# Layer-2 features from projected keys and queries in row blocks, one table of steps per batch, and earlier weight loads

## What is computed

```python
q = (x @ Wq + bq).reshape(B, S, H, hd).transpose(0, 2, 1, 3)
...
x_proj = jnp.einsum('bhsd,dm->bhsm', x, random_matrix)   # hd = 8, m = 32, H = 16
return (jax.nn.elu(x_proj) + 1.0) * INV_SQRT_M
...
kv = jnp.einsum('bhsm,bhsd->bhmd', k_prime, v)
k_sum = k_prime.sum(axis=2)
out = jnp.einsum('bhsm,bhmd->bhsd', q_prime, kv)
...   # divided by q_prime . k_sum, then @ Wo + bo
```

## Time and profile before

| | us |
|---|---|
| median of 3 runs | 527.77 |
| lowest, highest | 526.52, 531.72 |
| the profiled execution | 527.63 |
| its span, first to last instruction | 525.8 |
| TensorE busy | 481.0 |
| VectorE busy | 386.0 |
| ScalarE busy | 224.6 |
| POOL busy | 106.5 |

### The profile page before, as it was taken

How to read it: one execution, slowest core, us unless ns; L and a number is a source line. 1 busy time by engine, 2 the same in 40 slices (tenths; PEclk the granted TensorE clock), 3 DMA queues, 4 the chain that set the end, 5 groups by cost and what they waited for, 6 DMA issues and landing times. The chain is left out here.

```text
span 525.8 us, 7943 instructions
## 1 busy us (share of the span) xinstructions
PE 481.0 (91%) x2903; PEld 232.8 (44%) x2903; DVE 386.0 (73%) x994; ACT 224.6 (43%) x302; POOL 106.5 (20%) x101
## 2 busy tenths in 40 slices
PE   8889899999999999989979979999999999988772
PEld 3333233334333343333335545556557456545471
DVE  6398888887898888798629796974678466655553
ACT  2306657667766656656841222231332232233110
POOL 9880427006440010000100002000011001212020
PEclk9999999999999999999999999998999799879756
DMA  4854342224322333200132113112111000000000
GB/s 155 259 142 156 90 123 92 91 70 112 115 91 70 93 86 113 66 1 22 23 80 82 60 42 100 42 60 60 41 42 51 30 20 1 21 1 0 22 20 20
DMA packets 24878, 36.31 MB, mean 69 GB/s; under 512 B 2684, under 2 KB 16258, under 8 KB 24834
## 3 DMA queue, kind: packets, MB, share of 16 engines
q1 hardware_dynamic: 24840, 35.81, 23.3%
HBM read 24.07 MB, written 11.53 MB: 68 GB/s over the span
## 5 line engine op out<-in xcount | busy, mean ns | idle before, releaser
L1092 DVE TENSOR_REDUCE negmax<-psum 128x1 f32<-128x512 f32 x256 | 169.6, 687 | 34.0 <-PE psum L521 33.8
L805 ACT ACTIVATE probs<-psum 128x1024 f32<-128x1024 f32 x128 | 127.7, 1022 | 60.1 <-PE psum L537 57.7
L521 PE MATMUL psum<-KS,QS 125*128 125x512 bf16 x256 | 98.5, 385 | 7.4 <-DVE negmax L1092 4.1
L556 PE MATMUL psum<-probs,VA 128*32 128x256 f32 x1024 | 80.5, 390 | 0.4 <-ACT probs L805 0.4
L537 PE MATMUL psum<-QS,KS 128*128 128x512 bf16 x256 | 76.0, 380 | 0.1
L784 PE MATMUL psum<-xT,late 128*128 128x512 f32 x144 | 73.3, 634 | 0.0
L521 PEld LDWEIGHTS psum<-KS,QS 125*128 125x128 bf16 x256 | 24.5, 96 | 82.0 <-DVE negmax L1092 39.9
L448 POOL TENSOR_SCALAR var<-mv 128x4 f32<-128x4 f32 x16 | 4.3, 270 | 262.6 <-DVE mv L992 262.5
L915 ACT ACTIVATE QS<-psum 128x512 f32<-128x512 f32 x36 | 21.5, 597 | 65.2 <-PE psum L784 65.2
L771 PE MATMUL psum<-late,QS 128*128 128x128 f32 x288 | 40.6, 285 | 5.7 <-DVE QS L956 3.0
L1254 DVE SCALAR_TENSOR_TENSOR QS<-QS,psum 128x512 f32<-128x512 f32 x36 | 24.5, 680 | 26.1 <-ACT QS L915 26.1
(11 more groups left out here) (148 smaller groups left out, 590.0 us busy)
## 6 DMA issues: line engine op xcount, KB each, us to landing
stack_dram<-parts SPq DMA_DIRECT2D x24, 384.0 KB, 3.3
cw<-w_dram SPq DMA_DIRECT2D x32, 256.0 KB, 3.3
KS<-stack_dram SPq DMA_DIRECT2D x16, 288.0 KB
QS<-stack_dram SPq DMA_DIRECT2D x16, 288.0 KB
late<-in_late SPq DMA_DIRECT2D x8, 346.5 KB, 4.4
res<-in_x SPq DMA_DIRECT2D x4, 256.0 KB, 3.3
w_dram<-wT SPq DMA_DIRECT2D x4, 256.0 KB, 4.4
out_y<-KS SPq DMA_DIRECT2D x4, 256.0 KB, 2.2
```

Source lines behind the costliest of these rows:

```text
L521: mm(sm_bank(u)[:, :], QS[b % 2][0:KROW, h, qt * P:(qt + 1) * P], KS[b % 2][0:KROW, h, :], start=True, stop=True).then_inc(sm_full, 1)
L556: last_ = mm(ps[6][32 * j:32 * j + 32, q], VA[b % 2][:, kt, h, :], probs[:, n % 2, j, q], start=(kt == 0 and half == 0), stop=(kt == NT - ...
L805: fn(probs[:, n % 2, 2 * hf:2 * hf + 2, :], psum[:, 2 * hf:2 * hf + 2, :], ACT.Exp, scale=float(DH) ** -0.5).then_inc(exp_done, 1)
L1092: V.tensor_reduce(out=negmax[:, G % 4, i:i + 1], in_=sm_bank(u)[:, :], axis=X, op=ALU.max, negate=True).then_inc(sm_free, 1)
```

## The change

It does five things.

1. `wR`, `kb`, the split and the three bias DMAs go. Each batch gets `kp` and `qp`: keys and queries, projected (128x512 matmuls with `wk1`, `wq1`), evacuated by ScalarE with the bias into `kT`, `qT`.
2. K and Q tiles are made in pairs. K m and m+1: four matmuls, of 64 rows of `kT` with 256 columns of `rbd`, row block 0 into the first bank and 1 into the second, for two token tiles. Q m and m+1: two matmuls, each of the 32 rows of a head group, 128 features by 512 tokens.
3. ScalarE takes exp without bias and, as a second pass, identity with bias 1 into `kone` or `qone`; VectorE reads both from SBUF. A bank is free after ScalarE's second pass.
4. The rounds become one table `steps` for a batch, laid at 9 (n+1); where batches share a step, the later batch stands first. `x2T` is at 4, `kp` and `qp` at 5, K at 6 and 7, Q at 8 and 9, `KV` 9, `O` 10, `OT` 11, `AT` 12, `Y1` 14, `norm2` 15, `x3T` 17, `lg` 18, `ghT` 21, `Y2` 22, `norm3` 23. What is beyond step 35 is the tail, in this order, and crowded banks end with step 35.
5. The first three weight tiles are loaded right after `combine` of batch 0 (window 112).

```diff
-            wqT=D, wkT=D, wv1=D, wo1=D, rbd=H * M1, bq_rep=P, bk_rep=P, bv1_row=D, bo1_row=D, mask=HW,
+            wq1=D, wk1=D, wv1=D, wo1=D, rbd=H * M1, bq_col=1, bk_col=1, bv1_row=D, bo1_row=D, mask=HW,
...
-        wqR, wkR, bias_row = (probs[:, 0, i, :] for i in range(3))
...
+        qT, kT = probs[:, 0, 0, :], probs[:, 0, 1, :]
+        qone, kone = probs[:, 0, 2:4, :], probs[:, 1, 0:2, :]
...
-        a_round = (("K", 0, 0), ("AT", 1, 0), ("K", 0, 1), ("Y1", 1, 0), ("K", 0, 2), ("ghT", 2, 0), ("K", 0, 3),
-                   ("V", 0, 0), ("norm2", 1, 0), ("Y2", 2, 0), ("Q", 0, 0), ("Q", 0, 1), ("x3T", 1, 0), ("Q", 0, 2),
-                   ("norm3", 2, 0), ("lg", 1, 0), ("Q", 0, 3), ("KV", 0, 0), ("O", 0, 1), ("O", 0, 0), ("OT", 0, 1),
-                   ("OT", 0, 0))
-        round_at = (4, 4, 5, 5, 5, 6, 6, 7, 7, 7, 8, 8, 9, 9, 9, 10, 10, 11, 12, 12, 12, 12)
...
+        steps = ((0, "chunk", 0), (1, "norm1", 0), (4, "x2T", 0), (5, "kp", 0), (5, "qp", 0), (6, "K", 0), (6, "K", 1),
+                 (7, "K", 2), (7, "K", 3), (7, "V", 0), (8, "Q", 0), (8, "Q", 1), (9, "Q", 2), (9, "Q", 3), (9, "KV", 0),
+                 (10, "O", 1), (10, "O", 0), (11, "OT", 1), (11, "OT", 0), (12, "AT", 0), (14, "Y1", 0), (15, "norm2", 0),
+                 (17, "x3T", 0), (18, "lg", 0), (21, "ghT", 0), (22, "Y2", 0), (23, "norm3", 0))
+        for n in reversed(range(NB)):
+            for at, kind, c in steps:
+                beside[PAIRS * (n + 1) + at].append((kind, n, c))
...
-            for j in range(NB * EP):
-                if j == 12:
-                    sp.wait_ge(kb_done, 2)
-                    for i in range(3):
-                        sp.dma_start(bias_stack[i:i + 1, :, :], bias_parts[0:1, :, i, :]).then_inc(ks_ld, 16)
+                        if a == 0:
+                            for j in range(CW):
+                                load_weights(j)
+            for j in range(CW, NB * EP):
...
                 if kind == "K":
-                    mm(o[:, :], tile_of(m), wkR[:, :], start=True, stop=False)
-                    last_ = mm(o[:, :], onesb[:, 0:P], bias_stack[:, 0, :], start=False, stop=True)
+                    other = ("K", b, m + 1)
+                    wait_free(pe, other)
+                    for t in range(2):
+                        for r, out_ in enumerate((o, bank_of(other))):
+                            half = slice(64 * r, 64 * (r + 1))
+                            last_ = mm(out_[:, 256 * t:256 * (t + 1)], kT[half, (m + t) * P:(m + t + 1) * P],
+                                       c_["rbd"][half, 256 * r:256 * (r + 1)], start=True, stop=True,
+                                       tile_position=(64 * r, 0))
...
                 if kind == "Q":
-                    mm(o[:, :], wqR[:, m * P:(m + 1) * P], xT[:, b * T:(b + 1) * T], start=True, stop=False)
-                    last_ = mm(o[:, :], bias_stack[:, 1, m * P:(m + 1) * P], onesb[:, :], start=False, stop=True)
+                    other = ("Q", b, m + 1)
+                    wait_free(pe, other)
+                    for c, out_ in ((m, o), (m + 1, bank_of(other))):
+                        rows_ = slice(HW * c, HW * (c + 1))
+                        last_ = mm(out_[:, :], c_["rbd"][rows_, c * P:(c + 1) * P], qT[rows_, :], start=True, stop=True,
+                                   tile_position=(HW * c, 0))
...
-                    fn(ek_[:, i % 2, :], bank_of(u)[:, :], ACT.Exp, bias=minus1[:, 0:1]).then_inc(expk_done, 1)
+                    fn(ek_[:, i % 2, :], bank_of(u)[:, :], ACT.Exp)
+                    fn(kone[:, i % 2, :], bank_of(u)[:, :], ACT.Identity, bias=plus1[:, 0:1]).then_inc(expk_done, 1)
...
-                    V.scalar_tensor_tensor(out=KF[:, m, :], in0=ek_[:, i % 2, :], scalar=1.0, in1=bank_of(u)[:, :],
+                    V.scalar_tensor_tensor(out=KF[:, m // 2 * 2:m // 2 * 2 + 2, 256 * (m % 2):256 * (m % 2 + 1)], in0=ek_[:, i % 2, :], scalar=1.0, in1=kone[:, i % 2, :],
```

More of the change, by code:

```diff
@@ L96, in program @@
         cw = sb("cw", [P, CW, T])
-        onesb = sb("onesb", [3, T], BF16)
         warm_in = sb("warm_in", [P, T], BF16)
@@ L221, in program @@
-        round_at = (4, 4, 5, 5, 5, 6, 6, 7, 7, 7, 8, 8, 9, 9, 9, 10, 10, 11, 12, 12, 12, 12)
-        for n in range(NB):
-            w = PAIRS * (n + 1)
-            for at, kind in ((0, "chunk"), (1, "norm1"), (3, "x2T")):
-                beside[w + at].append((kind, n, 0))
-            if n + 1 < NB:
-                for (kind, back, c), at in zip(a_round, round_at):
-                    if n >= back:
-                        beside[w + at].append((kind, n - back, c))
+        steps = ((0, "chunk", 0), (1, "norm1", 0), (4, "x2T", 0), (5, "kp", 0), (5, "qp", 0), (6, "K", 0), (6, "K", 1),
[3 rows of a table added]
@@ L230, in program @@
+        for n in reversed(range(NB)):
+            for at, kind, c in steps:
+                beside[PAIRS * (n + 1) + at].append((kind, n, c))
         layer2 = [s for one in beside[NB * PAIRS:] for s in one]
         del beside[NB * PAIRS:]
-        crowded = {s for one in beside for s in one} | set(layer2)
-        for n in range(last, NB + 2):
-            layer2 += [(kind, n - back, c) for kind, back, c in a_round if 0 <= n - back < NB]
+        crowded = {s for one in beside for s in one}
@@ L237, in program @@
         uses = [[] for _ in range(8)]
-        in_misc = ("rope", "val", "max", "heads", "attnT", "proj", "resT", "gate", "combine", "wR", "kb", "x2T")
+        in_misc = ("rope", "val", "max", "heads", "attnT", "proj", "resT", "gate", "combine", "x2T")
         uses[MISC] = [s for one in [[("val", 0, 0), ("max", 0, 0)]] + slots for s in one if s[0] in in_misc]
@@ L246, in program @@
             uses[5].append(("y_e", b, 0))
-        bank_for = {"K": 2, "Q": 0, "V": 4, "KV": 5, "O": 5, "OT": 5, "AT": 7, "Y1": 4, "x3T": 7, "lg": 5, "ghT": 7, "Y2": 6, "x2T": 7}
+        bank_for = {"kp": 3, "qp": 1, "K": 2, "Q": 0, "V": 4, "KV": 5, "O": 5, "OT": 5, "AT": 7, "Y1": 4, "x3T": 7, "lg": 5, "ghT": 7, "Y2": 6, "x2T": 7}
         swap = 0
@@ L486, in _ @@
                 pool.wait_ge(init_pool, i + 1)
-            link(nc.gpsimd.memset(onesb[:, :], 1.0))
             nc.gpsimd.memset(VK[:, :, :, :], 1.0).then_inc(init_pool, 1)
```

77 lines of the change are left out of this document (39 added, 38 removed).

## The result

| | time, median | profiled execution | span | mean granted clock |
|---|---|---|---|---|
| before | 527.14 us (4 runs, 524.46 to 531.72) | 527.63 us | 525.8 us | 0.952 |
| changed | 521.47 us (4 runs, 519.22 to 523.43) | 519.63 us | 517.8 us | 0.926 |

The ratio is 0.9896, with a 95% interval of 0.9848 to 0.9944: 5.7 us are gained, where 14 were forecast. The number lies in the range of 505 to 527, but the forecast saw over twice the gain. Ratios are taken to runs of the kernel before on the same chip, and leave out runs over 1.5% above the fastest of their kernel.

The account below looks back on a forecast made before the run. It took TensorE matmul time to bound the expert stage and latency, one batch's chain of small steps, the tail; 19.0 us saved less 4.9 lost gives 14.1 less, 513.5, said as 514 us, range 505 to 527.

Parts of the forecast that it names:

- Row blocks overlap: K and Q pairs: row blocks run side by side like O's column blocks, 1.00 us a pair, gaining 9.8 us.
- row blocks don't overlap: Rival for K and Q pairs: 1.86 us a pair, time 525 us; chance 0.15.
- The expert stage: From the first gate_e to the last up_e: features, folded weights, sooner loads and table together save 19.0 us.
- Features and folded weights: Expert stage: pairs with projections save 9.8 us, dropping wR and kb saves 3.4 + 2.6 us.
- table and loads: Expert stage: sooner weights save 2.7 us; the new step table saves 2.4 and costs 0.4 and 1.5.
- the clock falls more often: Rival: each expert-stage pair brings a place at 1.2 GHz behind it, 19.8 us, time 533.3 us; chance 0.10.
- The tail is no worse: Rival: full clock in lg, Y2 and Y1 and room for gates in the tail, time 507 us; chance 0.18.
- The tail: After the last up_e, one batch's chain of small steps: five pieces together 4.9 us worse.
- third piece: Tail, KV 3 to attn: lg 2 now in between, 3.7 + 0.9 + 3.5 + 4.0 = 12.1 us, 2.3 worse.
- second piece: Tail, x2T 3 to KV 3: pairs at ScalarE's pace, 18.2 us instead of 23.5, 5.3 better.
- `KV` itself at 1.2 GHz in the tail: Rival: gaps from ScalarE's pace make KV 7.3 instead of 3.7 us, twice, time 521 us; chance 0.12.
- ScalarE's second pass: Extra identity per tile: covered in the expert stage; in the tail pairs follow at 2 x 1.2 us of ScalarE.

Follow-up runs that it names:

- e3: The kernel before with only the first three weight tiles loaded sooner; 523.32 us, ratio 0.9893.
- e4: The changed kernel's features (projections, pairs, two ScalarE passes, no folded weights) in the rounds and with the weight loads of the kernel before; 526.25 us, ratio 0.9863.
- a0: The changed kernel run once more, unaltered, which gives its second profile; 523.63 us, ratio 0.9928.
- e1: The changed kernel with only the tail's list put back in the order of the kernel before; 517.42 us, ratio 0.9774.
- e6: The changed kernel with full matmuls for the tail's pairs and the tail in the order of the kernel before; 509.97 us, ratio 0.9664.
- e5: The changed kernel with full 128-row matmuls for the tail's pairs, row blocks kept in the expert stage; 515.04 us, ratio 0.9748.
- e13: The changed kernel with only the tail's Q pairs as full 128-row matmuls, its K pairs still in row blocks; 513.61 us, ratio 0.9787.
- e9: The changed kernel with one full matmul, whose result is overwritten, ahead of each row-block pair of the tail; 522.26 us, ratio 0.9915.
- e7: The changed kernel without ScalarE's second pass; VectorE reads the tile from PSUM and the added 1 is left out; 528.66 us, ratio 0.999.
- e11: e6 with lg moved to PSUM bank 3 and short bf16 filler matmuls in TensorE's remaining tail gaps; 496.77 us, ratio 0.942.
- e14: The kernel before with only lg moved from bank 5 to PSUM bank 3; 527.66 us, ratio 1.0026.

## Why the prediction was right or wrong

**Row blocks overlap: right.** A pair is 1.05 to 1.06 us, forecast 1.00 from the column blocks of `O`. (By the 3.07 times of the Trainium skill, TensorE: Matmul & The Clock Gate, Part 3: Packing small matmuls, the estimate was 1.12: this trace lies between the two.) The rival "row blocks don't overlap" fell.

**The expert stage: right, and a little small.** Forecast -19.0; measured -24.3, and -21.1 in the second profile, which has 10.2 us at 1.2 GHz like before's. Step 11's `gate_e` starts 35.8 us after the stage's start instead of 46.0, so 10.2 sooner where some 9 were forecast; the weights alone are 2.7 of them in `e3`, as forecast. The last `up_e` ends at 419, forecast 422, although the stage began 2.5 us late. Single terms within the other 7.5 us were not measured one by one, but three profiles with the same 10.2 us at 1.2 GHz split the stage: 172.9 before, 159.1 in `e4`, 151.8 in `a0`. Features and folded weights are 13.8 of it, forecast 15.8; table and loads 7.3, forecast 3.2. Which step of the table gives the 4 more was not measured. The rival "the clock falls more often" was wrong for the expert stage: one place in the profile (L786 at 383.63, 3.30 us), 3.4 to 13.7 us at 1.2 GHz over the 13 profiles with row blocks in this stage, 0 to 17.1 over the five without. "The tail is no worse" fell with the 96.1 us.

**The tail: this is the step that failed.** Forecast +4.9, measured +13.5 between the marks and +13.8 to +16.0 by the table. Piece by piece, before, forecast, measured:

```
last up_e -> x2T 3     20.1    23.6    25.7    (419.0 to 444.75)
x2T 3 -> KV 3          23.5    18.2    19.3    (to 464.06)
KV 3 -> attn            9.8    12.1    16.8    (to 480.81)
attn -> x3T 3          10.6    16.0    17.1    (481.50 to 498.61)
the end                18.0    17.0    16.5    (to 515.1)
```

Every piece has the sign that was forecast. The waits that the new order makes were found in advance and sized well: the gate chain in a row ahead of `ghT` (5.06 us from `AT` to `ghT`, forecast 5.0), `lg` between `KV` and `O` (3.7, forecast 3.5). Changing the order back is worth 7.3 to 9.5 us (`e1`) and 7.6 (`e6` against `e5`); the pieces that the order makes add up to 3.5 + 2.3 + 5.4 - 1.0 = 10.2 in the forecast.

What failed is the full clock that the sum gives to `KV` 3 and to `O`, the terms 3.7 and 4.0 of the third piece, and with it the gain of 5.3 us that the second piece gives to the pairs. They do finish sooner there (19.3 us instead of 23.5), but the third piece pays it back: `KV` 3 takes 7.04 instead of 3.76, and from `O`'s start to `attn` it is 5.4 (475.45 to 480.81), as long as before, where the forecast had given `O` the full clock and 4.0 (by its own rows 5.42 less 1.77, so 3.65). In the first piece the same term measured 5.0 (432.03 to 437.04). These three are 3.3, 1.4 and 1.0 us of the 8.6 by which the tail was missed. The prediction had this as a rival, "`KV` itself at 1.2 GHz in the tail", with 0.12. Half of it happened: `KV` 3 did, `KV` 2 didn't (3.78 us; 4.46 in the second profile). Its time, 521, is close to the measured ones, but partly by luck, since the expert stage gained more than it assumed. The rival's reason was wrong as well. It named the gaps that ScalarE's pace leaves ahead of `KV`. The gaps are not enough: ahead of the last Q pair `e13` waits 0.99 us and `e9` 1.82, and both keep the clock for `KV` 3; the changed kernel waits 0.96 (1.46 in the second profile) and loses it. So the mistake in working was to take the time that a matmul takes as all that it does to the tail. The fair comparison is `e6`: with the order of before and full matmuls the tail is 85.0 us, as long as before's; and `e1`, the same with row blocks, 91.6. In the new order without the blocks (`e5`) it is 92.6, 7.5 longer than before's, where the forecast has 10.2 for the order. So the order was priced high enough; but where the forecast takes off 5.3 for the pairs, in blocks they added 6.3 and 8.5.

Why blocks of 32 rows ahead of `KV` go with the lower clock, and gate and expert matmuls between the blocks of the expert stage do not, is not shown. What is shown is the exchange: same order, nearly the same waits, only the Q pairs in full, and `KV` 3 goes from 7.04 to 3.66 us, the tail from 98.9 and 101.1 to 92.5, and the ratio from 0.9928 to 0.9787 (some 7 us; the intervals don't overlap).

**ScalarE's second pass: the pace was right, the sum around it was not.** The second K pair waits 2.42 us for it, as the forecast pace says. But a pair's own matmuls stand between the passes as well: from the end of the first pair to the start of the fourth are 9.8 us (452.27 to 462.05), where 7.8 were summed, which the first pair, 1.5 sooner than forecast, makes good in part. Without the pass the kernel is not faster but slower (`e7`). The pass lets go of the bank before VectorE has read it, and the longer wait of `e7` (4.33 us) fits that this is worth more than its 0.6 us. By the profiles the tail of `e7` is only 0.9 and 3.1 us longer, so not all of the 5.0 is explained. The Trainium skill (TensorEngine Tiling (Array Packing), PSUM Bottleneck) says that after a fourfold speedup by packing the copy out of PSUM may become the bottleneck and that both ScalarE and VectorE should be used for it. In the tail that is how it looks, with 2.42 us between the end of each first pair and the start of the second (behind the first Q pair with `x3T` 2 in between). The two engines were not the better choice here: giving the copy to ScalarE twice was faster, 523.63 us against 528.66 with ScalarE and VectorE once each.

**The attention stage: not in the prediction.** It ended 2.5 us later. Its profile has two falls of the clock to 1.2 GHz, near 25 and 66 us, which the one of before has not. `e11`, with the same code in this stage, has none and ends at 267.9, as before; `e3` and `e14`, with the layer-2 work of before, have one each and end at 268.6 and 268.9. So the later end goes with the falls, and neither is forced by the change or reserved to it. Over all profiles with the new features the stage ends at 269.5 to 270.0 with one fall and at 270.4 to 271.1 with two. Whether the change makes them more likely is open: 19 falls in 14 profiles with it, 2 in 4 without.

**The order of the errors.** From the profiled executions: expert stage 5.3 us better than forecast, tail 8.6 worse, attention 2.5 worse, behind the last mark 0.2 worse, together 6.0 worse; 513.5 + 6.0 = 519.5, near the execution's 519.63. The median lies 1.8 above that.

## What to carry to other kernels

In a stretch where TensorE waits often, ask of a new matmul form not only how long it takes but at which clock the work behind it runs: Q pairs of 1.06 us in the tail cost some 7 us against pairs of 1.79 (ratios 0.9928 and 0.9787; medians 523.63 and 513.61). When a list of steps is made by a rule, read the part that runs without cover by itself, since an order that is free beside full queues (`lg` behind `KV` in its bank, `ghT` before its gates are made) becomes waits there; here order, matmul form and one bank number together were worth 23 us on top of the change. And a short wait ahead of a long row of matmuls can cost more than its length: removing 3.4 us of waits gave 9.5, 8.2 of it in the tail.
